# First-layer weight splits of 14 of 24 quads stored to memory in the first batch and fetched in the second

## The reference, cut to what matters

```python
attn_out = softmax(q @ k.T * scale) @ v @ Wp + bp
cms_out  = gelu(attn_out @ cW1 + cb1) @ cW2 + cb2 + one_hot(target_codes)
concat   = concatenate([attn_out, cms_out], axis=-1)
modifier = gelu(concat @ mW1 + mb1) @ mW2 + mb2      # mW1: 1024 x 2048
out      = clip(x + cms_out + modifier, 0, 1)
# then, per sequence, expert e = stream[b]:
h = out + gelu(out @ W_down[e] + b_down[e]) @ W_up[e] + b_up[e]
y = layernorm(h) * ln_w[e] + ln_b[e]
```

## Time and profile before

| what | us |
|---|---|
| median of 3 runs | 1058.02 |
| the runs | 1055.14, 1153.18, 1058.02 |
| profiled execution, its own time | 1056.88 |
| its span, first to last instruction | 1055.1 |
| PE busy in it | 1039.8 |
| DVE busy | 784.4 |
| ACT busy | 532.1 |
| DMA moved | 101.61 MB, mean 96 GB/s |

### The profile page before, as it was taken

How to read it: one execution, slowest core, us unless ns; L and a number is a source line. 1 busy time by engine, 2 the same in 40 slices (tenths; PEclk the granted TensorE clock), 3 DMA queues, 4 the chain that set the end, 5 groups by cost and what they waited for, 6 DMA issues and landing times. The chain is left out here.

```text
span 1055.1 us, 13880 instructions
## 1 busy us (share of the span) xinstructions
PE 1039.8 (99%) x4921; PEld 867.1 (82%) x4921; DVE 784.4 (74%) x1364; ACT 532.1 (50%) x971; POOL 7.6 (1%) x18
## 2 busy tenths in 40 slices
PE   8999999999999999999999999999999999999997
PEld 7889878888888778888889887888888887888886
DVE  5436966776588898787766796777757889887798
ACT  4425874444255443433575387554435544334357
POOL 0000000000000000000000000000000000000001
PEclk9999999999999999999999999999999999999999
DMA  5700121110133232210854222312004322423152
GB/s 162 279 1 20 60 81 40 54 67 21 60 135 125 101 130 111 99 61 12 315 153 121 80 80 80 120 41 74 27 21 160 140 80 100 148 100 113 40 160 80
DMA packets 59326, 101.61 MB, mean 96 GB/s; under 512 B 3102, under 2 KB 38010, under 8 KB 55418
## 3 DMA queue, kind: packets, MB, share of 16 engines
q1 hardware_dynamic: 59168, 100.70, 27.9%
q10 hardware_dynamic: 90, 0.02, 0.0%
HBM read 79.74 MB, written 20.97 MB: 95 GB/s over the span
## 5 line engine op out<-in xcount | busy, mean ns | idle before, releaser
L220 PE MATMUL bank<-hid_hi,w_lo 128*128 128x512 f32 x512 | 201.1, 393 | 3.6 <-DVE acc L1138 2.6
L679 ACT ACTIVATE sbc<-sbc,bias 128x512 f32<-128x512 f32 x112 | 80.9, 725 | 240.0 <-DVE sbc L1113 175.2
L222 PE MATMUL bank<-hid_lo,w_hi 128*128 128x512 f32 x512 | 199.4, 389 | 0.0
L221 PE MATMUL bank<-hid_hi,w_hi 128*128 128x512 f32 x512 | 199.3, 389 | 0.0
L1138 DVE TENSOR_TENSOR acc<-bank,acc 128x512 f32<-128x512 f32 x224 | 153.8, 687 | 54.4 <-PE bank L222 54.2
L220 PE MATMUL bank<-ta_hi,w_lo 128*128 128x512 f32 x448 | 174.8, 390 | 0.0
L222 PE MATMUL bank<-ta_lo,w_hi 128*128 128x512 f32 x448 | 174.4, 389 | 0.0
L221 PE MATMUL bank<-ta_hi,w_hi 128*128 128x512 f32 x448 | 174.3, 389 | 0.0
L1113 DVE TENSOR_TENSOR sbc<-bank,sbc 128x512 f32<-128x512 f32 x144 | 98.1, 686 | 38.8 <-PE bank L222 38.6
L588 ACT ACTIVATE sbc<-bank 128x512 f32<-128x512 f32 x112 | 66.4, 595 | 112.6 <-PE bank L222 112.4
L1032 DVE TENSOR_TENSOR w_lo<-w_raw,w_hi 128x256 fp32r<-128x256 f32 (+1 forms) x176 | 93.7, 562 | 36.6 <-ACT w_hi L588 36.6
(11 more groups left out here) (225 smaller groups left out, 1548.5 us busy)
## 6 DMA issues: line engine op xcount, KB each, us to landing
w_raw<-in_L_cond_mW SPq DMA_DIRECT2D x48, 512.0 KB, 3.5
w_raw<-in_L_cond_cW SPq DMA_DIRECT2D x32, 512.0 KB, 4.4
pre_d<-sbc SPq DMA_DIRECT2D x10, 1024.0 KB, 3.9
sbc<-pre_d SPq DMA_DIRECT2D x10, 1024.0 KB, 7.3
x_raw<-in_x SPq DMA_DIRECT2D x4, 1024.0 KB, 5.6
e_raw<-in_L_cond_W_down SPq DMA_DIRECT2D x8, 512.0 KB, 5.4
e_raw<-in_L_cond_W_up SPq DMA_DIRECT2D x8, 512.0 KB, 4.4
out<-acc SPq DMA_DIRECT2D x16, 256.0 KB, 2.1
```

Source lines behind the costliest of these rows:

```text
L220: nc.tensor.matmul(dst, w_l, a_h, start=start, stop=False, **kw)
L221: nc.tensor.matmul(dst, w_h, a_h, start=False, stop=False, **kw)
L222: return nc.tensor.matmul(dst, w_h, a_l, start=False, stop=stop, **kw)
L679: nc.scalar.activation(dst, dst, ACT.Gelu, **kw).then_inc(g_done[key], 1)
```

## The change

In the first batch SP stores both parts of all seven slots of quads 2 to 7 and 16 to 23 (`KEPT`, 14 quads) to the new memory tensor `w1_d`, 1792 KB each. In the second batch those quads are not loaded raw and not split: `dve_s`, the ACT and DVE splits return at once, and SP fetches part 1 (A11, A12, S1, S2, high and low: 1024 KB) once product S2 of quad i-2 is done, and part 2 (A22, S3, S4: 768 KB) once product S4 of quad i-2 is done. PE waits for the fetches. `w1_hi` and `w1_lo` become the halves of one buffer, so that one store takes both; in memory the piece of each partition is 14 KB long, and the parts' pieces are 4 KB and 3 KB. ACT's write into a buffer in the first batch now also waits until the store of the quad that was in it has landed (`split_out`). Counts of split operations become `split_no`, those of landings `w1_landed`. The core of the diff (`proj_out` is renamed `split_out` throughout, and `g` becomes `n`, the split's number, in the waits of the split helpers):

```diff
+    KEPT = tuple(range(2, NQ)) + tuple(range(2 * NQ, QB))
+    w1_d = nc.dram_tensor("w1_d", (len(KEPT), P, 2, 7, 2, P), F32, kind="Internal").ap()
...
+        w1_both = [at(f"w1_both{i}", W1H + o * KB, [P, 2, 7, 2, P], F32R) for i, o in enumerate((18, 0))]
+        w1_hi = [t[:, 0, :, :, :] for t in w1_both]
+        w1_lo = [t[:, 1, :, :, :] for t in w1_both]
...
+        is_kept = lambda b, i: b > 0 and i in KEPT
...
             def first(i, which):
...
                 if which == 1:
-                    pe.wait_ge(w1_l1, 3 * g + 2)
+                    if is_kept(b, i):
+                        pe.wait_ge(w1_in[i % 2], w1_landed(b, i, 1))
+                    else:
+                        pe.wait_ge(w1_l1, 3 * n + 2)
...
             def second(i, which):
                 g = quad(b, i)
                 if which == 7:
-                    pe.wait_ge(w1_l2, 2 * g + 2)
+                    if is_kept(b, i):
+                        pe.wait_ge(w1_in[i % 2], w1_landed(b, i, 2))
+                    else:
+                        pe.wait_ge(w1_l2, 2 * split_no(b, i) + 2)
...
         def act_w1_first(act, b, i, part):
-            g = quad(b, i)
+            if is_kept(b, i):
+                return
+            g, n = quad(b, i), split_no(b, i)
...
+                if b == 0 and i - 2 in KEPT:
+                    act.wait_ge(split_out, w1_stored(i - 2))
...
+        def load_kept(sp, b, i, part):
+            sp.wait_ge(w1_in[i % 2], w1_landed(b, i, part) - 16)
+            if i >= 2:
+                sp.wait_ge(p6_mm if part == 1 else p3_mm, quad(b, i - 2) + 1)
+                if part == 2 and i < 4:
+                    sp.wait_ge(p4_mm, quad(b, i - 2) + 1)
+            sp.dma_start(kept_part(w1_both[i % 2][:, :, :, :, :], part).bitcast(F32),
+                         kept_part(w1_d[KEPT.index(i), :, :, :, :, :], part))\
+                .then_inc(w1_in[i % 2], 16)
+
+        def store_kept(sp, i):
+            sp.wait_ge(split_out, w1_stored(i) - 16)
+            sp.dma_start(w1_d[KEPT.index(i), :, :, :, :, :].rearrange("p h w k n -> p (h w k n)"),
+                         w1_both[i % 2][:, :, :, :, :].rearrange("p h w k n -> p (h w k n)").bitcast(F32)).then_inc(split_out, 16)
...
         def sync_mlp(sp, b):
             for it in range(QB + 2):
-                if it + 2 < QB:
-                    sp.wait_ge(w1_l2, 2 * quad(b, it) + 2)
+                if it + 2 < QB and not is_kept(b, it + 2):
+                    last = max(j for j in range(it + 1) if j % 2 == it % 2 and not is_kept(b, j))
+                    sp.wait_ge(w1_l2, 2 * split_no(b, last) + 2)
+                    if is_kept(b, it):
+                        sp.wait_ge(w1_in[it % 2], w1_landed(b, it, 2))
                     load_w1(sp, b, it + 2)
+                if b == 0 and it in KEPT:
+                    sp.wait_ge(w1_l2, 2 * it + 2)
+                    store_kept(sp, it)
+                if it + 2 < QB and is_kept(b, it + 2):
+                    load_kept(sp, b, it + 2, 1)
+                if 1 <= it < QB - 1 and is_kept(b, it + 1):
+                    load_kept(sp, b, it + 1, 2)
                 if has_l2(it):
...
```

More of the change, by code:

```diff
@@ L108, in build @@
         w2_lo = [at(f"w2_lo{i}", o + 40 * KB, [P, 2, 2, V], F32R) for i, o in enumerate((Y0, X0))]
-        w1_hi = [at(f"w1_hi{i}", W1H + o * KB, [P, 7, 2, P], F32R) for i, o in enumerate((18, 0))]
-        w1_lo = [at(f"w1_lo{i}", W1H + (o + 7) * KB, [P, 7, 2, P], F32R) for i, o in enumerate((18, 0))]
+        w1_both = [at(f"w1_both{i}", W1H + o * KB, [P, 2, 7, 2, P], F32R) for i, o in enumerate((18, 0))]
+        w1_hi = [t[:, 0, :, :, :] for t in w1_both]
+        w1_lo = [t[:, 1, :, :, :] for t in w1_both]
         s_f = at("s_f", S0, [P, 4, 2, P])
@@ L164, in build @@
             "wp_in", "bias_in", "codes_in", "experts_in", "bd_in"))
-        proj_out, x_in, xd_out, xr_in = sem("proj_out"), sem("x_in"), sem("xd_out"), sem("xr_in")
+        split_out, x_in, xd_out, xr_in = sem("split_out"), sem("x_in"), sem("xd_out"), sem("xr_in")
         aw_in = [sem(f"aw_in{s}") for s in range(3)]
@@ L206, in build @@
         quad = lambda b, i: QB * b + i
+        is_kept = lambda b, i: b > 0 and i in KEPT
+        split_no = lambda b, i: quad(b, i) - (sum(1 for j in KEPT if j < i) if b else 0)
+        kept_same = lambda b, i: sum(1 for j in KEPT if j < i and j % 2 == i % 2) if b else 0
+        w1_landed = lambda b, i, part=1: 16 * (QB // 2 * b + i // 2 + kept_same(b, i) + part)
+        w1_stored = lambda i: 64 + 16 * sum(1 for j in KEPT if j <= i)
         has_l2 = lambda i: 0 <= i < QB and phase_of(i) != 1
@@ L512, in first @@
                 elif which == 5:
-                    pe.wait_ge(w1_l1, 3 * g + 3)
+                    if not is_kept(b, i):
+                        pe.wait_ge(w1_l1, 3 * n + 3)
                     if i >= 2:
@@ L598, in act_w1_first @@
             if part == 0:
-                act.wait_ge(w1_in[i % 2], 16 * (g // 2) + 16)
+                act.wait_ge(w1_in[i % 2], w1_landed(b, i))
+                if b == 0 and i - 2 in KEPT:
+                    act.wait_ge(split_out, w1_stored(i - 2))
                 if i >= 2:
@@ L610, in act_w1_first @@
             else:
-                act.wait_ge(s_step, 4 * g + 3)
+                act.wait_ge(s_step, 4 * n + 3)
                 act_copy(w1_hi[i % 2][:, 2:4, :, :], sf[:, 0:2, :, :]).then_inc(w1_h1, 1)
         def act_w1_second(act, b, i):
-            g = quad(b, i)
+            if is_kept(b, i):
+                return
+            g, n = quad(b, i), split_no(b, i)
             if i >= 2:
@@ L618, in act_w1_second @@
             act_copy(w1_hi[i % 2][:, 4, :, :], raw_blocks(i)[3]).then_inc(w1_h2, 1)
-            act.wait_ge(s_step, 4 * g + 4)
+            act.wait_ge(s_step, 4 * n + 4)
             act_copy(w1_hi[i % 2][:, 5:7, :, :], (s_g if i == 1 else s_f)[:, 2:4, :, :]).then_inc(w1_h2, 1)
@@ L693, in act_hid @@
             else:
-                act.wait_ge(proj_out, 64)
+                act.wait_ge(split_out, 64)
             act_copy(hid_hi[reg][:, r % 2, c, t, :], sbc[:, i % 3, tile, :]).then_inc(hid_h[key], 1)
@@ L1044, in dve_s @@
         def dve_s(dve, b, i):
-            g = quad(b, i)
+            if is_kept(b, i):
+                return
+            g = split_no(b, i)
             a11, a12, a21, a22 = raw_blocks(i)
@@ L1050, in dve_s @@
                 dve.wait_ge(w1_l2, 2 * g)
-            dve.wait_ge(w1_in[i % 2], 16 * (g // 2) + 16)
+            dve.wait_ge(w1_in[i % 2], w1_landed(b, i))
             nc.vector.tensor_tensor(sf[:, 0, :, :], a21, a22, ALU.add).then_inc(s_step, 1)
@@ L1622, in expert_id, with kept_part @@
             return sp.value_load(exp_id[0:1, seq:seq + 1], min_val=0, max_val=E - 1)
+        def kept_part(t, part):
+            return (t[:, :, 0:4, :, :] if part == 1 else t[:, :, 4:7, :, :]).rearrange("p h w k n -> p h (w k n)")
+        def load_kept(sp, b, i, part):
[11 more added lines that the diff above has]
+                         w1_both[i % 2][:, :, :, :, :].rearrange("p h w k n -> p (h w k n)").bitcast(F32)).then_inc(split_out, 16)
         def load_w1(sp, b, i):
-            g = quad(b, i)
             src = (cw1[:, 0:KT, :], mw1[:, 0:KT, :], mw1[:, KT:2 * KT, :])[phase_of(i)]
@@ L1679, in sync_mlp @@
                 if it == QB and b + 1 == NBAT:
-                    sp.wait_ge(w1_l2, 2 * QB * NBAT)
+                    sp.wait_ge(w1_l2, 2 * split_no(NBAT - 1, QB))
                     load_piece(sp, b, 0)
@@ L1722, in sync_program @@
             for slot in range(2):
-                sp.dma_start(proj_hi[:, slot, :], aw_hi[slot][:, :].bitcast(F32)).then_inc(proj_out, 16)
-                sp.dma_start(proj_lo[:, slot, :], aw_lo[slot][:, :].bitcast(F32)).then_inc(proj_out, 16)
+                sp.dma_start(proj_hi[:, slot, :], aw_hi[slot][:, :].bitcast(F32)).then_inc(split_out, 16)
+                sp.dma_start(proj_lo[:, slot, :], aw_lo[slot][:, :].bitcast(F32)).then_inc(split_out, 16)
             sync_mlp(sp, 0)
@@ L1732, in sync_program @@
                 sp.wait_ge(p3_mm, QB * b)
-                sp.wait_ge(proj_out, 64)
+                sp.wait_ge(split_out, 64)
                 half = KT * V // 2
```

## The result

| | before | changed |
|---|---|---|
| median | 1056.58 us (4 runs) | 1068.63 us (4 runs: 1065.73 to 1069.13) |
| profiled execution, span | 1056.88, 1055.1 us | 1065.73, 1064.0 us |

A forecast was written before the change was run, and what follows sets the result against it. The prediction took PE to bound the kernel and summed 7.9 - 2.5 + 0.2 + 0.2 = +5.8 us on the profiled 1056.88, so 1062.7 us. Its own range was 1059 to 1066 (chance 0.50), the 8-in-10 range 1053 to 1071.

The forecast's parts named there:

- rival (b): Second batch: slow reading back at 300 GB/s, 13 us instead of 7.9, 0.5 at the border; 1068.3 us; chance 0.15.
- Gain: Second batch: without the splits PE wins back what it lost to late DVE; 2.5 us, bounds 0 and 2.5.
- Quads 19 to 22: Second batch: the `pre_d` tile lands late behind part 2 and holds PE 1.0 us per iteration, 4.0 us in all.
- Quad 23: Second batch: two expert pieces also stand ahead of the `pre_d` tile; PE loses 3.9 us.
- The border of the second batch: load_w2(16) slips behind two kept parts, but the chain has room until about 867: no cost, bound 1 us.
- The lead-in: Start of the second batch: load_w2(0) goes behind part 1 of quad 2; 0.2 us, bounds 0 and 1.
- First batch: At its border, store 16 delays ACT's writing of quad 18's high parts; 0.2 us, bounds 0 and 4.
- rival (c): First batch: stores at half of 410 GB/s hold ACT 4.5 us longer, some 3.3 us more; 1066.0 us; chance 0.10.
- rival (a): Second batch: the burst lands by 5.3 us into the iteration, DVE never holds PE; 1054.8 us; chance 0.25.

The follow-up runs named there:

- e1: Changed kernel with both kept-part loads moved to the end of SP's list in each iteration; 1053.43 us, ratio 0.9978 to the kernel before.
- e2: Changed kernel with SP's wait for S4 left in place but part 2's transfer issued at the list's end; 1059.90 us, ratio 1.0034 to before.
- e8: Changed kernel with only part 2 and its wait for S4 moved to the end of SP's list; 1054.21 us, ratio 0.9981 to before.
- e3: Changed kernel with the first batch's stores only; the second batch loads raw weights and splits as before; 1057.69 us, ratio 1.0015 to before.
- e7: e1 with quad 16 no longer kept (13 quads); 1052.82 us, ratio 0.9968 to the kernel before.
- e6: e1 with the first batch's stores also moved to the end of SP's list; 1054.20 us, ratio 0.9992 to the kernel before.
- e5: Changed kernel with the two expert pieces at it = 22 issued behind the `pre_d` load instead of ahead; 1063.63 us, ratio 1.0084 to before.

## Why the prediction was right, and where its sizes were off

**Direction, mechanism and place were right.** The five waits stand at quads 19 to 23, behind DVE's wait for `sbc<-pre_d`; e1 removes them by order alone, and e2 and e8 part the wait from the bytes. The size was not right: I forecast +5.8 us, and the medians moved by 12. 1068.6 us is inside the range of 1053 to 1071, but above the 1059 to 1066 that I gave the forecast itself; it was the room left for rival (b) that took it in. By the table every cost came out larger than forecast (in the order below by 1.1, 2.6, 1.2, 0.8 and 0.3 us), and the gain, larger by 0.7, made up for little of it. Step by step:

**Gain.** Forecast 2.5 us, which was also my upper bound. e1 shows 3.3 (1.2 + 0.4 + 1.7). I had counted the named waits and one gap; late starts at the phases' border (0.4) and one near 657 us (0.2) were not counted. That no gain beyond PE's own losses was to be had held. DVE's busy time fell by 48.6 us where I forecast about 60; I had added mean durations, and the split rows already overlap (144 of 416 ns are 59.9, busy 54.6).

**Quads 19 to 22.** Forecast 4 x 1.0, measured 5.1 (1.45, 2.09, 0.74, 0.84). The tile came 6.7, 7.4, 6.0 and 6.1 us into the iteration, forecast 6.25; from part 2's issue that is 9.2, 9.9, 8.5 and 8.6 us, forecast 8.7. The burst's time was right to 0.4 us on average and too short for two of four. Rival (b) has the measured time (1068.3), and its rate can't be dismissed. Reckoned in its way (bytes over the time to landing less 1.65 us) the four bursts ran at 313, 287, 344 and 340 GB/s and quad 23's at 304, where the forecast amounts to 335 and (b) said 300; the five waits cost 11.6 us, nearer its 13 than my 7.9. But a steady slow transfer is not what the trace shows. Quad 19's burst in stretches of 1 us, after part 2's issue at 887.96, and the end of quad 20's:

```profile
889.00:890.00 1.00, 1.00 (x7) 0.80 (x6) 0.97 (x2) 0.97 (x2) 0.00 (x0) 1.00 0.72 83
890.00:891.00 1.00, 1.00 (x6) 0.84 (x5) 0.36 (x1) 0.11 (x1) 0.00 (x0) 1.00 0.71 221
891.00:892.00 1.00, 1.00 (x6) 0.84 (x5) 0.93 (x2) 0.00 (x0) 0.00 (x0) 1.00 0.98 396
892.00:893.00 1.00, 1.00 (x6) 0.81 (x5) 0.00 (x0) 0.00 (x0) 0.00 (x0) 1.00 1.04 408
893.00:894.00 1.00, 1.00 (x6) 0.84 (x5) 0.00 (x0) 0.00 (x0) 0.00 (x0) 1.00 1.19 465
...
916.00:917.00 1.00, 1.00 (x6) 0.84 (x5) 0.00 (x0) 0.00 (x0) 0.00 (x0) 1.00 1.08 459
917.00:918.00 1.00, 1.00 (x6) 0.81 (x6) 0.00 (x0) 0.00 (x0) 0.00 (x0) 1.00 0.54 213
918.00:919.00 1.00, 1.00 (x6) 0.71 (x4) 0.00 (x0) 0.00 (x0) 0.00 (x0) 1.00 0.00 0
```

In quad 19 two us pass at 83 and 221 GB/s, then it runs above 390. In quad 20, the slowest, no transfer started after 918.0, and yet the tile landed only at 919.7: there the time was lost at the end. One average, as in the earlier trace rows, hid that shape. The kept parts themselves were slower than forecast as well, and stayed hidden: in these iterations part 1 took 5.3 to 5.9 us to land (forecast 4), part 2 4.6 to 4.9 (forecast 3.6), and PE never waited for either.

**Quad 23.** Forecast 3.9, measured 6.5: the term with the largest error. Part 2 was issued at 974.68 and the tile landed at 987.5, 12.8 us later, where my steps give 11.6. PE stood idle for 4.8 us, 1.0 more than forecast, and then the clock, which I had not thought of, took its share. PE in order of time, then the same in stretches of 1 us:

```profile
988.89 0.79 PE L228 MATMUL bank<-hid_hi,w_lo 128*128 128x512 f32 x1 [4.77 <-DVE acc L1165]
989.48 0.63 PE L229 MATMUL bank<-hid_hi,w_hi 128*128 128x512 f32 x1
989.91 0.63 PE L230 MATMUL bank<-hid_lo,w_hi 128*128 128x512 f32 x1
...
991.62 0.57 PE L228 MATMUL bank<-tc_hi,w_both 128*128 128x512 f32 x1
992.02 0.40 PE L229 MATMUL bank<-tc_hi,w_both 128*128 128x512 f32 x1
...
988.00:989.00 1.00, 0.11 (x1) 0.11 (x1) 1.00 (x3) 0.00 (x0) 0.00 (x0) 0.79 1.10 349
989.00:990.00 1.00, 1.00 (x3) 0.81 (x4) 1.00 (x3) 0.53 (x1) 0.00 (x0) 0.50 0.99 311
990.00:991.00 1.00, 1.00 (x4) 0.81 (x3) 1.00 (x3) 0.53 (x2) 0.00 (x0) 0.50 0.15 49
```

The granted clock was at half (0.50, 1.2 GHz) as PE went on. The starts from 988.89 to 992.02, seven apart, took 3.13 us instead of 7 x 0.227 = 1.59: 1.5 us lost, of which a plain restart explains 0.1.

**The border of the second batch.** Forecast: nothing, bound 1 us, since the chain had room until about 867. Measured: e1 wins 1.7 us in iteration 18, the changed kernel 0.5, so 1.2 us. The step that failed is the landing of load_w2(16). ACT after, with its idle time, and above it SP's issue of that load and its KB and us to landing:

```profile
859.50 0.55 SPq L1678 DMA_DIRECT2D w_raw<-in_L_cond_mW  x1
...
w_raw<-in_L_cond_mW SPq DMA_DIRECT2D x1, 512.0 KB, 6.6
...
866.08 1.06 ACT L603 ACTIVATE w_hi<-w_raw 128x1024 fp32r<-128x1024 f32 x1 [6.54 <-DMA w_raw<-in_L_cond_mW]
867.05 1.33 ACT L700 ACTIVATE sbc<-sbc,bias 128x512 f32<-128x512 f32 x2
868.41 0.63 ACT L603 ACTIVATE hid_hi<-sbc 128x512 fp32r<-128x512 f32 x1
868.95 0.71 ACT L700 ACTIVATE sbc<-sbc,bias 128x512 f32<-128x512 f32 x1
869.69 1.15 ACT L603 ACTIVATE hid_hi<-sbc 128x512 fp32r<-128x512 f32 x2
```

This trace runs 2.3 us early there. The issue at 859.50 is 861.8 by the times of before, as forecast (861.5). But the landing at 866.1 is 868.4, and I had forecast 866: the load took 6.6 us, where my 861.5 to 866 gave it 4.5, about the 4.3 that it took before. Now two kept parts were under way ahead of it. The room was right: behind the load stand two gelus and a copy (867.05 to 869.0) before the gelu of the chain, which begins at 868.95, 2.87 us after ACT took up the load. It had been at 870.06, so ACT could take the load up as late as 867.2 by the times of before, my "about 867". It took it up at 868.4, and 1.2 us is what was lost.

**The lead-in.** Forecast 0.2, bound 1; measured 1.0. e1, which puts load_w2(0) ahead again, takes it away, and e8 brings 0.8 back. The same fault as at the border: behind part 1 the load took 6.3 us to land instead of 4.4, besides being issued 1.5 us later.

**First batch.** Forecast 0.2, measured 0.5 (e3 and e7 show it is store 16). The store landed 7.8 us after its issue, forecast 7.3, so rival (c), which had it 4.5 us later, did not come true. The bounds, 0 and 4, were wide; e6 reached 1.8 by making the store later.

**The rule of the Trainium skill** on the time of one DMA ("DMA: Bandwidth & Descriptors", section "Anatomy of one DMA") was rival (a)'s. That section gives its fit for one DMA issued from GpSimd, and the loads here are issued by SP, which the prediction does not say. The fit gives 7.4 us for the burst; the four took 8.5 to 9.9 us from part 2's issue to the tile's landing, so these traces don't support it for transfers issued one right behind the other. Rival (a) as such is refuted by the waits.

**What is missing** between the table's 11.1 us and the medians' 12 is not traced; single executions of either kernel differ by more than that (1055.1 to 1058.0 and 1065.7 to 1069.1), and the changed kernel's trace is of its fastest.

## What to carry to other kernels

Where a queue works in order, a load that must wait for a late event belongs behind every load that need not, even if the data path is half idle; here the same transfers in another order make the difference between 1.1% slower and 0.2% faster (e1). Relief for engines beside the bound is worth only the bound engine's own gaps, so sum these first. For a load that slips behind others, do not carry over the time that it took to land: here the same 512 KB took 6.6 us instead of 4.3, and 6.3 instead of 4.4. Add that landing to the instructions queued behind its first user, end to end up to the bound engine.

## What the runs showed that I had not expected

The price of a wait was not in proportion: waits of PE of 1.8 and 1.9 us (quad 20 of the changed kernel, quad 23 of e5) cost themselves and 0.3, while those of 2.8 us (e2) and 4.8 us went with some 3 us at half the granted clock, 1.2 GHz, and cost 1.9 and 1.7 us on top. And the same 1 MB tile behind the same two loads took between 7.2 and 8.5 us from issue (quads 21 and 20 of the changed kernel); no run shows what sets this.
